# Moving a load of x behind the spectral blocks, reordering copies in the opening chunks, shortening a taps operation and repeating products

## The chip, the cores and the metric

One core of one Trainium2 chip. The metric is the device time of one execution in microseconds: the median of the runs, 957.55 us before the change (three runs, 956.13 to 961.07). Names of engines: PE is TensorE's matmul, PEld its weight load, DVE is VectorE, ACT ScalarE, POOL GpSimd, SP SyncE (which issues the DMAs here).

## The reference

x has the shape (8, 64, 64, 64): batch, channels, two image axes. Two layers follow one another; each adds a convolution of the channel-normalised x and then a small mixture of experts.

```python
x = x + _L0_conv_ref(_ln_c(x), L0_conv_kernel_base)      # spectral: fft, 32x32 modes mixed over channels, inverse
t = _to_tokens(x)
t = t + _L0_ffn_ref(_ln_t(t), ...)                       # 8 experts, the best 2 per token, softmax-weighted
x = _from_tokens(t, x)
x = x + _L1_conv_ref(_ln_c(x), L1_conv_kernels)          # depthwise, 29x29 taps
t = _to_tokens(x)
t = t + _L1_ffn_ref(_ln_t(t), ...)
return _from_tokens(t, x)
```

## The kernel before, in words

One program, five instruction streams written out by hand, one for each engine; each runs in its own order and waits on semaphores. x stays in a region X of on-chip memory, 128 partitions by 256 token tiles of 64 channels. A region R3 and a region R1 hold what the stages need in turn.

**Start and spectral stage.** SyncE loads x twice at the start, by rows (for the statistics, into X) and by channels (for TensorE). TensorE transforms along one axis (line 1453) and the other (line 1470), 16 groups. The mixing stage multiplies the modes with 8 steps of 17 spectral matrices each: SyncE loads the raw pieces of a step (two DMAs a step, line 407), steps 0 to 2 when the transform has left the place free (waits at 402 to 405), later ones when an earlier step's low halves are made; ScalarE makes the high halves (line 1172), VectorE the low ones (line 747), TensorE multiplies (line 1492, up to six small matmuls for each matrix). Between the pieces of step 2 and those of step 3, SyncE waits until the last rows are measured and issues x once more, now in the layout by tokens, in four DMAs into X (line 414), since X is free from there on. After step 7 it issues the experts' weights (line 417). Then come transposes (line 1558), the inverse along one axis (line 1570) and along the other (line 1707); VectorE and GpSimd add its results onto X (lines 1069 and 561) and wait for x by tokens before the first one.

**Token stages.** Each layer handles its 256 tiles in 8 chunks of 32, a chunk in 16 pairs of tiles. A pair `p` of chunk `k`: TensorE computes the products of two tiles with seven experts (`expert_pair`, two matmuls of 448 columns for each tile, lines 1605 and 1606) into one of two PSUM areas; VectorE weighs them by the gates (`weigh_pair`, line 904); GpSimd adds the weighed parts of two pairs (lines 571 and 581); TensorE sums these four tiles with the residual (`sum_quad`, lines 1616 to 1625) and ScalarE copies each two such sums back to X (`copy_sum`, line 1291). Products of pair p+2 wait until pair p is weighed.

Beside the pairs of a chunk the next chunks are prepared, eight tiles (a quarter of a chunk) at a time: VectorE measures (`stats_part`, line 660); ScalarE normalises into one PSUM bank, in two halves of four tiles (`normalise`, line 1249), and takes the high half (line 1261); VectorE makes the low half (`low_parts`, line 844), and only then may ScalarE normalise the next quarter; TensorE turns the eight tiles (`turn_tokens`, line 1583); ScalarE copies the turned tokens out of PSUM (`copy_parts`, lines 1278 and 1279), and only then may TensorE turn the next quarter; TensorE computes the router's logits (`route`, lines 1593 and 1594); VectorE makes the gates in 15 steps (`gate_part`, lines 862 to 892). At which pair each of these happens stands in tables. For the opening chunk (chunk 0) of each layer they are

```python
START_NORMS = {1: (1, 2), 3: (1, 3), 5: (2, 0), 8: (2, 1), 12: (2, 2)}
START_LOWS = {1: (1, 1), 3: (1, 2), 5: (1, 3), 7: (2, 0), 10: (2, 1), 14: (2, 2)}
START_TURNS = {0: (1, 0), 3: (1, 1), 5: (1, 2), 7: (1, 3), 9: (2, 0), 13: (2, 1)}
FIRST_ROUTE = (2, 5, 7, 9)
```

where (1, 2) is quarter 2 of chunk 1. ScalarE's order within a pair is set by `start_chunk` (line 1318), TensorE's by the one at line 1647. Before chunk 0 of each layer its own gates are made (VectorE's 15 steps in a row), while TensorE has done the products of pair 0 and, after the turn of quarter (1, 0), those of pair 1.

At pair 13 of layer 0's opening chunk VectorE also makes the low half of the convolution's taps (`taps_low`, line 946, its instruction at line 950), from `taps_f32` and the copy that ScalarE made (line 1316). SyncE then writes the taps to DRAM in 128 shifted copies, paced by the pairs weighed (line 426). Each half holds 2412 columns in rows of 38; the 29x29 taps lie in one region of it, and all the rest is zero.

**Convolution** (455 to 685 us): a loop over channels, TensorE at line 1692. Layer 1's token stage follows, and the results are stored.

Of the kernel before, what the change touches and what calls it, by code (L numbers as in the profile page):

```python
# [15 lines left out]
B, C, H, W = 8, 64, 64, 64  # L16
# [6 lines left out]
NT = HB * WB * B  # L23
BO, BP, B2 = 2, 2, 2
BH, BQ = 2, 4
KS = 29
NE = 8
KRING = 3
PITCH = 38
# [4 lines left out]
CENTRE = 31 * PITCH + 23  # L34
TAP_SCALE = 256.0
# [32 lines left out]
def metaformer(nc, x_chan, x_rows, x_tok, spec_pairs, spec_last, dft, dft16, inv_h, inv_c, ident, ident16,  # L68
               experts0, experts1, rank, taps, out):
    ctx = ExitStack()  # L70
    with ctx:
# [3 lines left out]
        def sem(name):  # L75
            return ctx.enter_context(nc.semaphore(name))
# [6 lines left out]
        X = sb("X", NT * C)  # L83
# [63 lines left out]
        taps_f32 = R1[:, 5120:5120 + TAPS]  # L147
        taps_16 = R1[:, 7680:7680 + TAPS // 2].bitcast(F16)
# [20 lines left out]
        x_in = sem("x_in")  # L169
        piece_measured = sem("piece_measured")  # L170
# [98 lines left out]
        START_NORMS = {1: (1, 2), 3: (1, 3), 5: (2, 0), 8: (2, 1), 12: (2, 2)}  # L269
# [2 lines left out]
        START_GATES = {9: (0, 1), 10: (2, 3), 11: (4, 5), 12: (6, 7), 13: (8, 9), 14: (10, 11), 15: (12, 13, 14)}  # L272
        START_PARTS = (2, 3, 4, 4, 5, 6, 7, 8)
        START_EXP = 13
        NORM_AHEAD, LOW_AHEAD, TURN_AHEAD = 3, 3, 2
        COPY_AT, SUM_LAG, QUAD_LAG = 1, 2, 3
        GATES_AT = {7: (0, 1), 8: (2, 3), 9: (4, 5), 10: (6, 7), 11: (8, 9), 12: (10, 11), 13: (12, 13, 14)}
# [12 lines left out]
        UNITS = ((0, 0, 32), (0, 32, 64), (1, 0, 32), (1, 32, 64), (2, 0, 64), (3, 0, 64))  # L290
# [69 lines left out]
        def _(sp):  # L360
# [40 lines left out]
            for t in range(NSTEP):  # L401
                if t < 3:
                    sp.wait_ge(c_dft, 20 + 2 * t)
                else:
                    sp.wait_ge(k_low, 2 * (t - 2))
                for r in BLOCKS:
                    sp.dma_start(k_raw[t % 3][r], spec_pairs[:, PER_STEP * t:PER_STEP * t + PER_STEP, :]
                                 ).then_inc(k_in[t % 3], 16)
                if t == 2:

                    sp.wait_ge(piece_measured, len(UNITS))
                    for i in range(4):
                        n = NT * C // 4
                        sp.dma_start(X[:, i * n:(i + 1) * n], x_tok[:, i * n:(i + 1) * n]).then_inc(x_in, 16)

            wait_c_dft_low(sp, 32)
            sp.dma_start(raws_at[0], experts0).then_inc(raw_in, 16)

            sp.wait_ge(inv2, 32)
            for r in BLOCKS:  # L420
# [236 lines left out]
        def _(dve):  # L657
# [288 lines left out]
            def taps_low():  # L946

                dve.wait_ge(taps_step, 1)
                r = BLOCKS[1]
                dve.scalar_tensor_tensor(out=taps_16[r], in0=taps_f32[r], scalar=TAP_SCALE, in1=taps_16[r],  # L950
                                         op0=ALU.mult, op1=ALU.subtract).then_inc(taps_step, 1)

            def plane_stats(lo, hi):
# [167 lines left out]
        def _(act):  # L1121
# [117 lines left out]
            def normalise(layer, k, q, j, tiles=range(8)):  # L1239

                n = layer * NCHUNK + k
                if 0 in tiles:
                    if j == 0:
                        act.wait_ge(tok_step, (n + 1) * TOK_STEPS)
                    if layer or j or k:
                        act.wait_ge(tok_low, n * 4 + j)
                for t in tiles:
                    at = 8 * j + t
                    last = act.activation(xn_psum[:, t * C:(t + 1) * C], X[:, bass.ds(k * CT * C + at * C, C)],  # L1249
                                          ACT.Identity, bias=small[2 * q][:, at:at + 1],  # L1250
                                          scale=small[2 * q + 1][:, at:at + 1])
                if 7 not in tiles:
                    return
                last.then_inc(tok_normed, 1)
                if layer or k:
                    act.wait_ge(across, n * 4 + j - 3)
                act.wait_ge(tok_normed, n * 4 + j + 1 - 4 * layer)
                take_high(j, xn_psum)
# [11 lines left out]
            def copy_parts(layer, k, q, j):  # L1270

                n = (layer * NCHUNK + k) * 4 + j
                act.wait_ge(across, n + 1)
                if layer or not isinstance(k, int) or k >= 2:
                    act.wait_ge(summed, (layer * NCHUNK + k - 2) * NOCT + j + 1)
                src = bank[4 + j % 2] if layer and k == 0 else bank[4]
                at = slice(8 * j * P, 8 * (j + 1) * P)
                act.copy(u[q][:, at].bitcast(F32), src)
                act.copy(vh[q][0:64, at].bitcast(F32), src[0:64]).then_inc(parts_copied, 1)
# [38 lines left out]
            def start_chunk(layer):  # L1318
                for p in range(NPAIR):
                    if p % 4 == COPY_AT and p >= 4 * SUM_LAG:  # L1320
                        copy_sum(layer, 0, p // 4 - SUM_LAG)
                    if p in START_NORMS:
                        k, j = START_NORMS[p]
                        normalise(layer, k, k % 2, j, range(0, 4))
                    if p - 1 in START_NORMS:
                        k, j = START_NORMS[p - 1]
                        normalise(layer, k, k % 2, j, range(4, 8))
                    if p in START_TURNS:
                        k, j = START_TURNS[p]
                        copy_parts(layer, k, k % 2, j)  # L1330
                    if p == 2:
                        root_seed(layer, 2, 0)
                    if not layer and p == 10:
                        taps_high()
                    if p == START_EXP:
                        exp_second(layer, 1)
                    if p == ROOT_AT:
                        root_seed(layer, 3, 1)
# [43 lines left out]
            for g in range(32):  # L1382
                if g in POOLED:
                    n = POOLED.index(g)
# [60 lines left out]
        def _(pe):  # L1445
# [149 lines left out]
                if j == 3:  # L1595
                    mm.then_inc(logits_ready, 1)

            def expert_pair(layer, k, q, p):
                n = (layer * NCHUNK + k) * NPAIR + p
                if not (isinstance(k, int) and k == 0 and layer == 0 and p < 2):  # L1600
                    pe.wait_ge(y_used, n - 1)
                for i in range(2):
                    t = 2 * p + i
                    dst = pair[p % 2][:, i * EC:i * EC + EW]
                    pe.matmul(dst, u[q][:, t * P:(t + 1) * P], wa[:, 0:EW], start=True, stop=False)  # L1605
                    mm = pe.matmul(dst, vh[q][:, t * P:(t + 1) * P], wb[:, 0:EW], start=False, stop=True)  # L1606
                mm.then_inc(y_ready, 1)
# [39 lines left out]
            def start_chunk(layer):  # L1647
                for p in range(NPAIR):
                    if p % 2 == 0 and p >= 2 * QUAD_LAG:
                        sum_quad(layer, 0, 0, p // 2 - QUAD_LAG)  # L1650
                    expert_pair(layer, 0, 0, p)
                    if p in START_TURNS:
                        k, j = START_TURNS[p]
                        turn_tokens(layer, k, k % 2, j)
                    if p in FIRST_ROUTE:
                        route(layer, 1, 1, FIRST_ROUTE.index(p))
# [135 lines left out]
```

## Time and profile before

| what | us |
|---|---|
| median of three runs | 957.55 |
| profiled execution, its own time | 955.84 |
| its span (first to last instruction) | 954.1 |
| TensorE busy (matmuls) | 850.6, 89% |
| VectorE busy | 774.4, 81% |
| GpSimd busy | 567.5, 59% |
| ScalarE busy | 506.9, 53% |
| granted TensorE clock, mean | 0.936 |

All views come from the one profiled execution; times in them count from the span's start. "Granted clock" 1.00 is 2.4 GHz, 0.50 is 1.2 GHz. In a timeline a row is the start, the length, the engine, the line, the operation, what it writes and reads, the shapes and the count of merged instructions; in brackets how long the engine was idle before and what ended that. "Issue" stands for time in which an engine waited for nothing that the profile shows. A busy share is an average over stages with different limits, so the stages that the change touches are read one by one.

### The profile page before, as it was taken

How to read it: one execution, taken by the hardware profiler on the slowest of the kernel's cores; microseconds unless marked ns; L12 is line 12 of the kernel's file. 1: busy time of each engine (PE TensorE's matmuls, PEld its weight loads, DVE VectorE, ACT ScalarE, POOL GpSimd, SP SyncE). 2: the span in 40 equal slices, each digit the busy share in tenths (PEclk: the TensorE clock that was granted, in tenths of full speed). 3: DMA queues.
4: the chain of work that ended last, by engine and by line, in shares of the span. 5: the costliest groups of instructions: out<-in, count | busy, mean ns of one | idle time of the engine just before them, and what ended most of it. 6: DMA issues, size and time to landing. Idle time of an engine off the chain costs nothing.

```text
span 954.1 us, 24392 instructions
## 1 busy us (share of the span) xinstructions
PE 850.6 (89%) x9482; PEld 699.1 (73%) x9482; DVE 774.4 (81%) x1421; ACT 506.9 (53%) x1051; POOL 567.5 (59%) x504
## 2 busy tenths in 40 slices
PE   6997888677999998996899999999658999999998
PEld 6996877645676666654899999999635666667665
DVE  5768698888999989999787677774787999998884
ACT  2467485786667766211444444444168676676511
POOL 3780203157798887796654334330216888889888
PEclk9997577988999999999899999999959999999999
DMA  9997100103777776683787877888000010101101
GB/s 377 355 294 258 50 1 2 40 15 153 281 311 300 301 300 274 280 323 122 265 282 253 286 264 259 274 275 264 13 1 13 33 46 24 45 24 45 46 40 49
DMA packets 48291, 163.09 MB, mean 171 GB/s; under 512 B 9424, under 2 KB 9936, under 8 KB 46032
## 3 DMA queue, kind: packets, MB, share of 16 engines
q1 hardware_dynamic: 48208, 161.96, 46.7%
q8 instruction: 55, 0.90, 0.4%
q14 instruction: 28, 0.23, 0.1%
HBM read 93.46 MB, written 68.49 MB: 170 GB/s over the span
## 4 chain that ended last, share of the span: by engine, by line
PE 50%; DVE 31%; POOL 6%; issue 5%; DMA 3%; ACT 3%; SPq 1%; POOLq 0%; DVEq 0%; ACTq 0%
PE pair L1692 23%; DVE R L904 11%; PE pair L1619 5%; PE pair L1605 5%; PE pair L1606 4%; DMA X<-x_rows 3%; PE pair L1616 3%; DVE R L844 3%; PE pair L1492 3%; POOL R L571 3%; DVE R L660 2%; PE pair L1583 2%; DVE R L833 2%; DVE work L660 2%; ACT pair L1249 1%
## 5 line engine op out<-in xcount | busy, mean ns | idle before, releaser
L904 DVE TENSOR_TENSOR R<-pair,R 128x896 f32<-128x896 f32 x256 | 275.1, 1082 | 41.8 <-PE pair L1606 40.6
L571 POOL TENSOR_TENSOR R<-R 128x768 f32<-128x768 f32 x128 | 231.9, 1812 | 85.8 <-DVE R L904 76.7
L1692 PE MATMUL pair<-R 128*128 (+4 forms) x2880 | 226.8, 242 | 9.8 <-DVE R L982 9.2
L1692 PEld LDWEIGHTS pair<-R 128*128 128x128 f16 x2880 | 223.9, 98 | 12.9 <-issue 10.5
L1249 ACT ACTIVATE pair<-X,work 128x64 f32<-128x64 f32 x480 | 166.7, 394 | 97.1 <-DVE R L844 94.6
L1605 PE MATMUL pair<-work,R 128*128 128x448 f16 x512 | 185.0, 361 | 22.4 <-DVE R L904 20.9
L1606 PE MATMUL pair<-work,R 128*128 128x448 f16 x512 | 184.4, 360 | 0.0
L581 POOL TENSOR_TENSOR R<-R 128x512 f32<-128x512 f32 x128 | 164.9, 1288 | 10.0
L997 DVE COPY R<-R 128x1152 f32<-128x1152 f32 x64 | 93.1, 1455 | 64.9 <-PE pair L1692 64.3
L1367 ACT COPY R<-R 128x1152 f32<-128x1152 f32 x64 | 81.9, 1282 | 117.4 <-PE pair L1692 117.4
L1619 PE MATMUL pair<-R,ident_sb 128*128 128x256 f32 x496 | 128.4, 381 | 0.0
L623 POOL TENSOR_TENSOR R<-X,work 128x1024 f32<-128x1024 f32 x15 | 43.9, 2929 | 103.5 <-DVE R L988 90.4
L1605 PEld LDWEIGHTS pair<-work,R 128*128 128x128 f16 x512 | 50.7, 99 | 73.7 <-DVE R L904 42.3
L1619 PEld LDWEIGHTS pair<-R,ident_sb 128*128 128x128 f32 x496 | 95.0, 191 | 13.1
L660 DVE BATCH_NORM_STATS2 work<-X 128x6 f32<-128x128 f32 x384 | 84.9, 282 | 14.4 <-DMA X<-x_rows 14.4
L1616 PE MATMUL pair<-X,inv_h_sb 128*128 128x256 f32 x248 | 79.7, 403 | 0.0
L1291 ACT ACTIVATE X<-pair 128x512 f32<-128x512 f32 x62 | 36.0, 580 | 73.8 <-PE pair L1625 73.8
L1606 PEld LDWEIGHTS pair<-work,R 128*128 128x128 f16 x512 | 50.9, 99 | 30.7 <-issue 2.0
L1583 PE MATMUL pair<-ident_sb,R 128*128 128x128 f16 x512 | 42.9, 232 | 33.9 <-DVE R L844 27.1
L1583 PEld LDWEIGHTS pair<-ident_sb,R 128*128 128x128 f16 x512 | 36.1, 104 | 48.2 <-DVE R L844 30.4
L1453 PE MATMUL pair<-dft_sb,R 128*128 128x68 f32 x256 | 56.1, 422 | 9.1 <-DMA R<-x_chan 9.1
L1453 PEld LDWEIGHTS pair<-dft_sb,R 128*128 128x128 f32 x256 | 55.2, 333 | 9.3 <-issue 8.9
(137 smaller groups left out, 1292.7 us busy)
## 6 DMA issues: line engine op xcount, KB each, us to landing
taps_halves<-R SPq DMA_DIRECT2D x128, 458.5 KB, 3.3
R<-taps_halves SPq DMA_DIRECT2D x64, 917.0 KB, 4.8
X<-x_tok SPq DMA_DIRECT2D x4, 2048.0 KB, 17.8
out<-X SPq DMA_DIRECT2D x15, 512.0 KB, 2.6
R<-spec_pairs SPq DMA_DIRECT2D x16, 272.0 KB, 5.4
X<-x_rows SPq DMA_DIRECT2D x4, 1024.0 KB, 10.6
R<-x_chan SPq DMA_DIRECT2D x4, 1024.0 KB, 13.7
X<-x_rows SPq DMA_DIRECT2D x2, 2048.0 KB, 27.3
```

What stands on the lines that cost most here:

```text
L571: pool.tensor_tensor(pr[:, :, 192:384], pr[:, :, 0:192], pr[:, :, 192:384], ALU.add).then_inc(half_ready, 1)
L581: pool.tensor_tensor(w, pr[:, :, 192:320], pr[:, :, 320:448], ALU.add).then_inc(quarter_ready, 1)
L660: return dve.bn_stats(out_.rearrange("p t k -> p (t k)"), rows.rearrange("p t c -> p c t"))
L904: dve.tensor_tensor(pr.rearrange("p t (e c) -> p t e c", c=C), pair[p % 2][:, :].rearrange("p (t e c) -> p t e c", t=2, c=C)[:, :, 0:NE - ...
L1249: last = act.activation(xn_psum[:, t * C:(t + 1) * C], X[:, bass.ds(k * CT * C + at * C, C)], ACT.Identity, bias=small[2 * q][:, at:at + 1 ...
L1453: mm = pe.matmul(c_dft_bank(n)[:, j * 68:(j + 1) * 68], xb[:, (4 * n + j) * P:(4 * n + j + 1) * P], dft_sb[:, :], start=True, stop=True)
L1583: mm = pe.transpose(out_[:, t * P:(t + 1) * P], parts[j][:, t * P:(t + 1) * P], ident16_sb[:, :])
L1605: pe.matmul(dst, u[q][:, t * P:(t + 1) * P], wa[:, 0:EW], start=True, stop=False)
L1606: mm = pe.matmul(dst, vh[q][:, t * P:(t + 1) * P], wb[:, 0:EW], start=False, stop=True)
L1616: pe.matmul(bank[7][:, 256 * half:256 * (half + 1)], ident_scaled, X[:, bass.ds((k * NQUAD + g) * 256, 256)], start=True, stop=False)
L1619: pe.matmul(bank[7][:, 256 * half:256 * (half + 1)], ident_sb[:, :], w[:, :, j, :], start=False, stop=False)
L1692: mm = pe.matmul(acc[:, y0:y1, x0:x1, :], blocks[i % 2][:, ks, 2 - y, 1 - x, :], src[:, y0 + y:y1 + y, x0 + x:x1 + x, :], start=(ks == 0 a ...
```

## The change

Four edits. SyncE issues the four DMAs of x by tokens after all spectral pieces and the experts' weights, no longer between steps 2 and 3. In the opening chunks ScalarE does the second half of a normalisation and the copy of turned tokens before the first half of the next normalisation, no longer after it. `taps_low` covers the 29x29 region alone (64 partitions by 29 rows of 29, rows 38 apart). TensorE writes the same products of pair 0 five times over, and those of pairs 11, 13 and 15 twice, in the opening chunk of both layers; the results are the same and the last writing signals.

```diff
+        TIMES = {0: 5, 11: 2, 13: 2, 15: 2}
...
-                if t == 2:
-
-                    sp.wait_ge(piece_measured, len(UNITS))
-                    for i in range(4):
-                        n = NT * C // 4
-                        sp.dma_start(X[:, i * n:(i + 1) * n], x_tok[:, i * n:(i + 1) * n]).then_inc(x_in, 16)
 
             wait_c_dft_low(sp, 32)
             sp.dma_start(raws_at[0], experts0).then_inc(raw_in, 16)
+            sp.wait_ge(piece_measured, len(UNITS))
+            for i in range(4):
+                n = NT * C // 4
+                sp.dma_start(X[:, i * n:(i + 1) * n], x_tok[:, i * n:(i + 1) * n]).then_inc(x_in, 16)
...
                 r = BLOCKS[1]
-                dve.scalar_tensor_tensor(out=taps_16[r], in0=taps_f32[r], scalar=TAP_SCALE, in1=taps_16[r],
+                first = CENTRE - KS // 2 * (PITCH + 1)
+                f32, f16_ = (m[r, first:first + KS * PITCH].rearrange("p (x y) -> p x y", y=PITCH)[:, :, 0:KS]
+                             for m in (taps_f32, taps_16))
+                dve.scalar_tensor_tensor(out=f16_, in0=f32, scalar=TAP_SCALE, in1=f16_,
                                          op0=ALU.mult, op1=ALU.subtract).then_inc(taps_step, 1)
...
-                    if p in START_NORMS:
-                        k, j = START_NORMS[p]
-                        normalise(layer, k, k % 2, j, range(0, 4))
                     if p - 1 in START_NORMS:
                         k, j = START_NORMS[p - 1]
                         normalise(layer, k, k % 2, j, range(4, 8))
                     if p in START_TURNS:
                         k, j = START_TURNS[p]
                         copy_parts(layer, k, k % 2, j)
+                    if p in START_NORMS:
+                        k, j = START_NORMS[p]
+                        normalise(layer, k, k % 2, j, range(0, 4))
...
-            def expert_pair(layer, k, q, p):
+            def expert_pair(layer, k, q, p, times=1):
...
-                for i in range(2):
+                for i in [*range(2)] * times:
...
-                    expert_pair(layer, 0, 0, p)
+                    expert_pair(layer, 0, 0, p, TIMES.get(p, 1))
```

## Rows read from the trace of the kernel before

**Rows 1.** The page, chain of waits that ended last, shares by engine.

```profile
PE 50%; DVE 31%; POOL 6%; issue 5%; DMA 3%; ACT 3%; SPq 1%; POOLq 0%; DVEq 0%; ACTq 0%
```

**Rows 2.** TensorE in the mixing stage: timeline; then waits of 84 to 102 us (us, times, longest).

```profile
82.50 3.88 PE L1492 MATMUL pair<-R 128*128 128x16 f16 x143 [1.50 <-DVE R L729]
89.23 3.56 PE L1492 MATMUL pair<-R 128*128 128x16 f16 x128 [2.85 <-issue]
...
101.25 13.49 PE L1492 MATMUL pair<-R 128*128 128x16 f16 x487 [0.70 <-issue]
...
PE pair L1492 <- issue: 4.2, 4, 2.8
```

**Rows 3.** DMA queues in 62 to 80 us: packets, MB, share of 16 engines.

```profile
q8 instruction: 1, 0.02, 0.4%
```

**Rows 4.** The loads of x by tokens, by source line; the experts' load, SyncE's timeline.

```profile
L414 SPq DMA_DIRECT2D X<-x_tok x4: 432/436/584, 56.4 to 58.0; - x4
...
DMA to landing us min/median/max: 11.1/17.8/26.8
...
96.02 0.52 SPq L417 DMA_DIRECT2D R<-experts  x1
```

**Rows 5.** TensorE's timeline, the turn at pair 5 of each opening chunk.

```profile
204.28 0.61 PE L1583 MATMUL pair<-ident_sb,R 128*128 128x128 f16 x8 [2.35 <-ACT R L1279]
...
721.09 0.61 PE L1583 MATMUL pair<-ident_sb,R 128*128 128x128 f16 x8 [3.36 <-ACT R L1279]
```

**Rows 6.** VectorE's waits, 203.5 to 217 and 717 to 735 us (total, times, longest); timeline.

```profile
DVE R L844 <- ACT R L1261: 2.4, 2, 1.3
DVE R L904 <- PE pair L1606: 1.6, 3, 0.7
...
DVE R L904 <- PE pair L1606: 3.3, 3, 2.1
...
722.95 0.69 DVE L844 TENSOR_TENSOR R<-pair,R 128x512 f16<-128x512 f32 x1 [1.27 <-ACT R L1261]
```

**Rows 7.** Busy time by stretch: PE, PEld, DVE, ACT, POOL, granted clock, DMA share, GB/s.

```profile
190.00:200.20 10.20, 6.70 (x44) 3.68 (x45) 9.28 (x18) 7.42 (x21) 3.01 (x2) 0.50 0.23 49
...
231.00:237.80 6.80, 4.66 (x48) 3.53 (x49) 5.29 (x12) 3.95 (x10) 4.62 (x4) 0.50 0.99 385
...
688.40:715.60 27.20, 14.37 (x145) 9.19 (x146) 24.11 (x64) 16.68 (x43) 5.34 (x14) 0.50 0.00 1
```

**Rows 8.** First products of both layers: TensorE's timeline; chain of waits (start, us).

```profile
192.37 1.03 PE L1583 MATMUL pair<-ident_sb,R 128*128 128x128 f16 x8 [4.14 <-DVE R L844]
...
707.61 1.04 PE L1583 MATMUL pair<-ident_sb,R 128*128 128x128 f16 x8 [3.50 <-DVE R L844]
...
212.09 0.19 PE pair L1605
...
710.12 0.93 DVE R L904
```

**Rows 9.** VectorE's timeline, first addition onto x by tokens.

```profile
151.68 0.69 DVE L1069 TENSOR_TENSOR X<-X,pair 128x512 f32<-128x512 f32 x1 [1.63 <-PE pair L1707]
```

**Rows 10.** VectorE's timeline, chunk 1 of each layer: weighing of pairs 0 and 2.

```profile
233.03 1.09 DVE L904 TENSOR_TENSOR R<-pair,R 128x896 f32<-128x896 f32 x1
...
239.61 1.09 DVE L904 TENSOR_TENSOR R<-pair,R 128x896 f32<-128x896 f32 x1 [2.47 <-PE pair L1606]
...
746.55 1.09 DVE L904 TENSOR_TENSOR R<-pair,R 128x896 f32<-128x896 f32 x1
...
751.23 1.09 DVE L904 TENSOR_TENSOR R<-pair,R 128x896 f32<-128x896 f32 x1 [1.34 <-PE pair L1606]
```

**Rows 11.** Timelines of VectorE and GpSimd at the low half of the taps.

```profile
224.75 3.59 DVE L950 SCALAR_TENSOR_TENSOR R<-R 64x2412 f16<-64x2412 f32 x1
...
224.00 1.81 POOL L571 TENSOR_TENSOR R<-R 128x768 f32<-128x768 f32 x1 [0.41 <-DVE R L904]
225.89 3.57 POOL L581 TENSOR_TENSOR R<-R 128x512 f32<-128x512 f32 x1
```

## The prediction

> **What bounds the kernel now.** I read the chain of waits first. It has no single owner: TensorE holds half of it, VectorE a third, and 5% is "issue", time in which an engine stood for no reason that the profile names [rows 1]. So I went to the three places that the diff touches, each by its own timeline.
>
> The first is the stage that mixes the spectral blocks (line 1492, 82.5 to 114.7 us). TensorE runs it without competition, but it stands four times, each time for "issue": 4.2 us in all, of which 2.85 are the first, at 86.38, and 0.70 the last; the two between share some 0.6 [rows 2]. From the end of one stand to the next there are 128 matmuls, with their weight loads 256 instructions, and the queue named "instruction" moves packets of 0.02 MB [rows 3]. I read the stands as a block of instructions that comes late. The 2.85 fell while x by tokens (four transfers, issued at 56.4 to 58.0, the last landing 26.8 us after its issue, so near 84.8) and the spectral pieces held up behind it were still in flight; the small ones fell beside spectral pieces alone [rows 2, 4].
>
> The second is the opening chunk of each layer (from 187 and 702 us). There ScalarE normalises four columns, copies the turned tokens, and normalises four more; TensorE waits 2.35 us (layer 0) and 3.36 us (layer 1) for the copy at line 1279 before the turn at pair 5 [rows 5]. VectorE, which paces the chunk, then waits for TensorE's products, three times in each layer: 1.6 us in all in layer 0, 3.3 in layer 1, besides twice for ScalarE's normalised columns, 2.4 in layer 0 and about as much in layer 1 [rows 6].
>
> The third is the granted clock. It is 0.5 (1.2 GHz) in 190 to 200 us, 231 to 237.8 and 688.4 to 715.6 [rows 7]. Before the first fall TensorE had run out of work after pair 0 and stood 4.14 us in all [rows 8].
>
> **The change, part by part.**
>
> *x by tokens behind the blocks.* SyncE's queue now issues the five pairs of pieces of steps 3 to 7 and the experts first, then x. The experts went out at 96.02 [rows 4]; the pieces come a little sooner, so x starts near 95.5 and lands 20 to 28 us later (8 MB; its last transfer took 26.8 with other pieces in between). The first reader needs it at 151.68 [rows 9]: some 28 us of cover, cost nothing; without that cover VectorE's additions would be late one for one. The wait on the measured rows, moved along, is over long before, and behind x on the queue stand only the taps, which wait for the end of the inverse stage.
> What it gives: the 2.85. What it costs: x now flies while TensorE mixes and asks for a block every 3.56 us. With the stall gone, requests fall near 97.8, 101.4, 105.0 and 108.5; the last would show only near the stage's end, so I count three and a half. No row shows a block fetched by a fast-running TensorE beside x alone. The ends: 0 (x's big transfers leave gaps), or 2.85 each, as beside x's tail. I take 0.70, the nearest row: the worst under well-filled queues without the jam of x and the pieces held up behind it. Stands after: 0.6 + 3.5 × 0.70 = 3.05 against 4.2, **a gain of 1.1**; the ends are a gain of 3.6 (0.6 left) and a loss of 7.8 (0.6 + 4 × 2.85 = 12.0).
> On this the Trainium skill has a rule, in "Runtime: NRT & Kernel Launch", section Instruction fetch mechanics: instructions come in blocks of 256, the next while the present one runs, and crossing a block costs little because it is mostly hidden. The spacing in this trace agrees with the 256; the 2.85 speaks against "hidden". By that rule of the Trainium skill the stage would not change at all, and the sum below would have 1.1 less of gain.
>
> *Products of pair 0 five times.* 16 more products; one takes 0.19 us of the chain at 2.4 GHz [rows 8], so 3.0 us in layer 0, in the 4.14 us in which TensorE waits for the turn: nothing on the path. In layer 1, at 1.2 GHz and so at twice that for one, 16 × 0.375 = 6.0 us, from 704.1 (707.61 less the 3.50 of waiting) to 710.1; the turn could go at 707.61, and VectorE, held by the gates, weighs pair 0 from 710.12 [rows 8]. If the clock rises during these 20 dense products, they end near 708 and cost nothing, as I take it; if not, pair 1 comes some 0.6 us late. The faster clock that follows gives little: VectorE waits for ScalarE and its own statistics there, at most 0.2.
>
> *Copies ahead of the first four columns* (pairs 3 and 5 only; at the other pairs the two do not meet). The work of ScalarE stays the same and so do the ends of its normalisations, but TensorE gets the copy some 1.4 us sooner, so turn, route, sum and the products of pairs 6, 8 and 10 move up. In layer 0 the three waits for TensorE, 1.6, go, and 0.4 of the second wait for ScalarE, since that copy no longer stands behind a normalisation that waits for VectorE: **2.0**. In layer 1 3.3 go; next late is ScalarE with the columns of chunk 2, which VectorE would meet 0.9 too early: 2.4. Ends: nothing in either layer, or all of the waits for TensorE and half of those for ScalarE, 2.8 and 4.5.
>
> *Pairs 11, 13 and 15 twice.* 4 × 0.19 = 0.76 us each. TensorE has slack there, since VectorE's gates come later than its products, but in layer 1 pair 14 comes behind two repeats and would be about 0.35 late once VectorE is 2.4 sooner. So **2.05** are left of layer 1.
>
> *Taps from their region.* 64 × 841 elements in place of 64 × 2412. The instruction took 3.59 us from 224.75, but GpSimd's addition at line 571, begun at 224.00, lasted 1.81, to 225.81, and its next one took 3.57, to 229.46, just past VectorE's end at 228.34 [rows 11]: the two engines took turns. So 1.06 was waiting and 2.53 work; 841 / 2412 of that is 0.88. GpSimd is at the same point of its own work in the new order, so I keep the 1.06: **a gain of 1.65**, up to 2.7 if the wait goes too, and 1.0 if the 29 short rows cost twice as much per element.
>
> *The clock at 231.* VectorE finishes the gates sooner, and TensorE has repeats at pairs 13 and 15: the stands that came before the fall grow shorter. I take it that the clock stays at 2.4 GHz. From the weighing of the next chunk's pair 0 to that of pair 2 it takes 239.61 − 233.03 = 6.58 us in layer 0 and, at full clock, 751.23 − 746.55 = 4.68 in layer 1 [rows 10]: **a gain of 1.9**, or nothing.
>
> *Sum.* 1.1 + 2.0 + 2.05 + 1.65 + 1.9 = 8.7. The chunks after the opening ones and the convolution start from these points and keep their lengths, so nothing takes it back. The profiled execution took 955.84 (span 954.1): 947.1. It lies 1.7 below the median of the runs, 957.55, which is what is compared: **948.8 us**.
>
> **Rivals.**
> *x stands in front of TensorE's instructions.* If a fetch has to wait for all that is queued on the engines, the one asked near 97.8 comes with x, at 116 to 122, and TensorE stands 15 to 20 us. The rest gives 7.6 and the old stands 3.6: from 11.2 us of standing the change loses; at 17.5 it ends 6.3 slower, at 963.9. For it: the 2.85 ended only as the held-up pieces landed. Against: a fetch came in at its time while x alone filled the queues from 62 to 80 (one packet on the instruction queue there [rows 3]) and TensorE ran on. Chance 0.05.
> *Every block as late as the worst*: a loss of 7.8 against 7.6 of gains, 957.8, no change. Chance 0.10.
> *The copies give nothing*, because ScalarE's normalisations, whose ends stay, set VectorE's pace: 4.05 less, 952.8. For it: the first wait for ScalarE in each layer stays as it is [rows 6]. Against: the waits behind them name TensorE. Chance 0.13.
> *The stand was no fetch* and the mixing keeps its length: 949.9. The equal spacing is against it. By the Trainium skill's rule on fetches, above, this is what should come. Chance 0.12.
>
> **How the numbers follow.** The forecast has 0.60. Its own ends (mixing 3.6, taps 2.7, or no gain from the clock and one copy) give 945 to 953. A difference of 0.5%, 4.8 us, is about what a measurement tells from none: below 952.8 is faster, above 962.3 slower. Faster: nearly all of the forecast, the fourth rival, half of the third: 0.76. Slower: the first, 0.05. The rest, 0.19, is the same. For 8 in 10 I take 944.5 to 956.5, which leaves out the first rival and the second.
>
> **What would show it.** Right: no long issue stand near 86, several under 1 us between 97 and 112, line 1492 ending a little before 114; x landing before 125; no wait of TensorE for line 1279 above 1 us; line 950's successor under 2.2 us; clock 1.0 from 226 on, and the two chunks' first weighings to third ones equally long. Wrong: a stand of TensorE of several us after 97, a wait for x at line 1069, or VectorE's waits for line 1606 replaced by as long ones for line 1261.

## The result, and the profile after

The changed kernel takes 960.4 us (median of 12 runs, 957.56 to 961.93); the kernel before, on the same chips, 957.33 (12 runs). The ratio is 1.0027 with a 95% interval of 1.0016 to 1.0038: slower by 0.3%, which is within the 0.5% that the prediction counted as no change, where it forecast 948.8 and a gain. The profiled execution took 960.74 (span 958.8), 4.7 us of span more than before.

The chain of waits has the same owners as before [rows 1], with a little more "issue":

```profile
PE 51%; DVE 29%; POOL 6%; issue 6%; ACT 4%; DMA 3%; SPq 1%; POOLq 0%; DVEq 0%; ACTq 0%
```

TensorE's timeline in the mixing stage (line 1494 after), then the stage's row in the list of waits (us in total, times, longest); they answer to [rows 2]:

```profile
82.94 3.82 PE L1494 MATMUL pair<-R 128*128 128x16 f16 x143 [2.26 <-DVE R L728]
87.51 3.57 PE L1494 MATMUL pair<-R 128*128 128x16 f16 x128 [0.74 <-issue]
91.25 3.56 PE L1494 MATMUL pair<-R 128*128 128x16 f16 x128 [0.17 <-issue]
96.07 3.58 PE L1494 MATMUL pair<-R 128*128 128x16 f16 x128 [1.26 <-issue]
103.37 3.79 PE L1494 MATMUL pair<-R 128*128 128x16 f16 x128 [3.72 <-issue]
109.84 3.79 PE L1494 MATMUL pair<-R 64*64 64x16 f16 x128 [2.69 <-issue]
116.05 3.58 PE L1494 MATMUL pair<-R 128*128 128x16 f16 x128 [2.41 <-issue]
121.16 2.91 PE L1494 MATMUL pair<-R 128*128 128x16 f16 x103 [1.52 <-issue]
...
PE pair L1494 <- issue: 12.5, 7, 3.7
```

The 2.85 of before is gone, as foreseen, but now every block of 128 matmuls is late, and the four that fall beside x stand 3.72, 2.69, 2.41 and 1.52 us. The stands grew from 4.2 us to 12.5. The granted clock is not behind it: it is 0.51 in 83.5 to 114 us before and 0.53 after.

What flies beside them: SyncE's timeline, and the landings of x by tokens (line 416), answering to [rows 4].

```profile
94.89 0.52 SPq L412 DMA_DIRECT2D R<-experts  x1
95.45 2.26 SPq L416 DMA_DIRECT2D X<-x_tok  x4
...
DMA to landing us min/median/max: 10.5/17.1/23.3
```

The DMA view by queue (packets, MB, share of 16 engines), for 96.1 to 100.8, 100.8 to 101.5 and 97.5 to 118 us:

```profile
q1 hardware_dynamic: 270, 1.70, 98.0%
...
q1 hardware_dynamic: 16, 0.26, 87.5%
q8 instruction: 1, 0.02, 9.7%
...
q1 hardware_dynamic: 674, 8.58, 100.0%
q8 instruction: 3, 0.05, 1.0%
```

These rows show the mechanism; the starts of the single packets are read from the same trace. TensorE enters a new block at 96.07. No packet of the instruction queue begins until 100.8; the next one begins at 100.87, and the stand ends 2.50 later, at 103.37. The three after it begin at 107.46, 113.60 and 118.70, and their stands end 2.38, 2.45 and 2.46 later. So beside x a block is ready about 2.45 us after its packet begins, and since a block runs 3.56, the packet must begin within about 1.1 of TensorE's entry into the block before it, or TensorE stands. Beside x it begins 4.8, 4.1, 3.8 and 2.65 after that entry: 4.8 + 2.5 − 3.58 is the 3.72 of the first stand.

From the mixing to the end, as the difference to the same point of before (the end of TensorE's mixing, or the start of a weighing at line 903, line 904 before):

| point | after minus before, us |
|---|---|
| mixing ends | +9.33 |
| inverse stages, first weighing of layer 0 | +8.79 |
| pair 8 of layer 0 | +7.18 |
| pairs 10 to 13 of layer 0 | +7.64 |
| pair 14 of layer 0 (behind the taps) | +6.00 |
| chunk 1 of layer 0, pair 2 | +5.38 |
| first weighing of layer 1 | +5.84 |
| pair 6 of layer 1 | +4.12 |
| pair 14 of layer 1 | +4.69 |
| end of the span | +4.72 |

One stage loses 9.33; all the rest together gains 4.6.

The taps (line 952), VectorE's timeline and the weighing behind it, answering to [rows 11]:

```profile
232.39 1.95 DVE L952 SCALAR_TENSOR_TENSOR R<-R 64x841 f16<-64x841 f32 x1
234.38 1.09 DVE L903 TENSOR_TENSOR R<-pair,R 128x896 f32<-128x896 f32 x1
```

In layer 0's opening chunk, waits of 212.3 to 225 us, answering to [rows 6], and TensorE's and VectorE's timelines at pair 10:

```profile
DVE R L843 <- ACT R L1263: 1.9, 2, 1.1
DVE R L903 <- PE pair L1608: 1.2, 1, 1.2
...
PE pair L1618 <- ACT X L1293: 0.8, 1, 0.8
...
221.94 0.67 PE L1618 MATMUL pair<-X,inv_h_sb 128*128 128x256 f32 x2 [0.83 <-ACT X L1293]
...
224.50 1.09 DVE L903 TENSOR_TENSOR R<-pair,R 128x896 f32<-128x896 f32 x1 [1.18 <-PE pair L1608]
```

Two of VectorE's three waits for products are gone. The third, at pair 10, has grown, from 0.70 to 1.18. ScalarE makes the copy of sums (line 1293, before: 1291) between the two halves of a normalisation, in both kernels. It comes 7.72 us later than before (at 221.21, where it came at 213.49), while VectorE at pair 8 is only 7.18 later. TensorE now waits 0.83 for it with its next sum, where it did not wait before, and the products stand behind that sum.

In layer 1 the turn at pair 5 still waits 1.87 us for the copy, where it waited 3.36 [rows 5]:

```profile
725.45 0.61 PE L1585 MATMUL pair<-ident_sb,R 128*128 128x128 f16 x8 [1.87 <-ACT R L1281]
```

The windows (busy time of PE, PEld, DVE, ACT, POOL, granted clock, DMA share, GB/s), answering to [rows 7]:

```profile
190.00:199.90 9.90, 8.16 (x134) 6.04 (x131) 8.28 (x21) 6.43 (x18) 0.00 (x0) 1.00 0.43 97
199.90:210.00 10.10, 6.71 (x52) 3.55 (x52) 8.97 (x17) 8.09 (x23) 3.57 (x3) 0.83 0.15 30
...
237.00:239.10 2.10, 0.00 (x0) 0.00 (x0) 2.00 (x5) 2.10 (x7) 1.35 (x2) 1.00 0.99 393
239.10:242.50 3.40, 3.35 (x45) 2.49 (x46) 2.66 (x6) 1.17 (x3) 1.96 (x3) 0.50 1.00 385
...
727.00:731.00 4.00, 4.00 (x20) 2.22 (x20) 2.33 (x5) 3.91 (x11) 3.52 (x4) 0.57 0.00 0
```

Since layer 0's opening chunk comes 8.8 us later now, the stretch that answers to 190 to 200.2 of before is about 199 to 209. The clock is low there too, but later and for a shorter time: 3.4 us, from 205.0 to 208.4, where it was 10.2. The fall at the end of the chunk is shorter as well (3.4 us) but still there. TensorE's timeline shows what comes before it:

```profile
239.15 0.17 PE L1595 MATMUL pair<-work,R 128*128 128x8 f16 x1 [2.69 <-DVE R L891]
```

TensorE stands 2.69 us, until VectorE has made the gates (line 891), and right behind that, from 239.1, the clock is 0.50. In layer 1 it falls once more at 727, as it did before the change at the same place (at 722.5):

```profile
722.50:725.80 3.30, 3.30 (x17) 2.06 (x16) 1.09 (x3) 2.48 (x7) 2.34 (x2) 0.50 0.00 0
```

### The profile page after: what moved, and what is told of

Its sections match the earlier page's. It is cut to its first block, busy times and chain, and to the rows that moved or that the text cites. A ratio compares the mean times of both kernels' runs of the same rounds, so it can differ in the third digit from the quotient of the medians.

```text
span 958.8 us, 24504 instructions
## 1 busy us (share of the span) xinstructions
PE 857.9 (89%) x9538; PEld 702.2 (73%) x9538; DVE 771.4 (80%) x1421; ACT 506.4 (53%) x1051; POOL 566.8 (59%) x504
## 4 chain that ended last, share of the span: by engine, by line
PE 51%; DVE 29%; POOL 6%; issue 6%; ACT 4%; DMA 3%; SPq 1%; POOLq 0%; DVEq 0%; ACTq 0%
PE pair L1694 24%; DVE R L903 11%; PE pair L1621 5%; PE pair L1607 5%; PE pair L1608 4%; DMA X<-x_rows 3%; PE pair L1618 3%; PE pair L1494 3%; POOL R L570 3%; DVE R L843 3%; DVE R L659 2%; PE pair L1585 2%; DVE R L832 2%; DVE work L659 2%; ACT pair L1251 2%
## 5 line engine op out<-in xcount | busy, mean ns | idle before, releaser
L1607 PE MATMUL pair<-work,R 128*128 128x448 f16 x540 | 194.4, 360 | 20.5 <-DVE R L903 18.9
L1608 PE MATMUL pair<-work,R 128*128 128x448 f16 x540 | 193.9, 359 | 0.0
L1607 PEld LDWEIGHTS pair<-work,R 128*128 128x128 f16 x540 | 53.4, 99 | 73.7 <-DVE R L903 39.4
L1608 PEld LDWEIGHTS pair<-work,R 128*128 128x128 f16 x540 | 53.6, 99 | 33.7 <-issue 2.7
```

## The experiments

Theory of the first runs: x in flight delays TensorE's instruction blocks, and that alone makes the change a loss. Its rival: the stands come from what else was changed, or from the pieces and experts that x no longer holds up.

**e1, the move of x alone** (the kernel before, with line 414's block behind the experts):

```diff
-                if t == 2:
-                    sp.wait_ge(piece_measured, len(UNITS))
...
             sp.dma_start(raws_at[0], experts0).then_inc(raw_in, 16)
+            sp.wait_ge(piece_measured, len(UNITS))
+            for i in range(4):
...
```

> The kernel before with the load of x moved behind the spectral pieces and the experts, and nothing else. Theory (x in flight starves TensorE of instructions): the mixing stage shows the same row of stands as the changed kernel, about 12 us in all in place of 4.2, it ends near 123.5 instead of 114.6, and nothing later takes it back: 8 to 9 us slower than before, ratio near 1.009. Rival (the stands come from elsewhere, x moved costs nothing): ratio 1.000, mixing ends near 114.

Measured: 964.46 us against 957.93, ratio 1.0063 (1.0043 to 1.0083), 6 us slower. Waits of the mixing stage and TensorE's timeline beside x:

```profile
PE pair L1490 <- issue: 11.8, 7, 3.2
...
101.41 3.79 PE L1490 MATMUL pair<-R 128*128 128x16 f16 x128 [3.17 <-issue]
107.89 3.80 PE L1490 MATMUL pair<-R 64*64 64x16 f16 x128 [2.69 <-issue]
114.37 3.58 PE L1490 MATMUL pair<-R 128*128 128x16 f16 x128 [2.68 <-issue]
```

The move by itself makes the stands and the whole loss, a little less than the 8 to 9 us expected: the mixing ends 7.65 later and the span 6.85.

**e2, everything but the move of x** (the changed kernel, x issued between steps 2 and 3 as before):

```diff
+                if t == 2:
+                    sp.wait_ge(piece_measured, len(UNITS))
+                    for i in range(4):
...
```

> The changed kernel with the load of x put back between the pieces of steps 2 and 3; the three edits of the opening chunks stay. Theory: the mixing stage is that of before (4.2 us of stands, the first near 2.9), and the opening chunks keep what the trace of the changed kernel shows, 3.4 us in layer 0 and 1.1 in layer 1: about 4.1 us faster than before, ratio near 0.996. Rival (the repeats or copies cost what they give and the trace misleads): ratio 1.000.

Measured: 953.45, ratio 0.9945 (0.992 to 0.9969), 5.3 us faster. Its profiled execution had late blocks of its own (3.31 at the same place as before, then 1.54 and 2.62 beside pieces and experts), which shows that the place of before is not safe either; even so, from the first weighing of layer 0 to the end it gains 3.1 us of span, where the changed kernel gains 4.1.

**e3, x behind the mixing** (the changed kernel; SyncE waits for the last mixed product before it issues x):

```diff
             sp.dma_start(raws_at[0], experts0).then_inc(raw_in, 16)
+            sp.wait_ge(mixed, NMIX)
             sp.wait_ge(piece_measured, len(UNITS))
```

> The changed kernel with one more wait ahead of the load of x: it starts when the last spectral product is written. Theory: in the mixing stage only the stands beside the spectral pieces stay, under 2 us in all, it ends near 112; x flies beside the transposes and the first inverse, where TensorE waits for copies anyway, lands near 133 and is needed near 148; about 6.5 us faster than before, ratio near 0.993. Rival (TensorE is short of instructions there whatever flies): stands of over 8 us in all, ratio near 1.003. Second rival (the cost only moves into the stages behind): mixing ends near 112 but the first inverse ends no earlier than with x in its old place, ratio near 0.996 or above.

Measured: 951.99, ratio 0.9923 (0.9894 to 0.9953), 7.4 us faster than before. TensorE's timeline in the mixing, and the DMA queues of 101.1 to 114 us:

```profile
91.36 3.56 PE L1495 MATMUL pair<-R 128*128 128x16 f16 x128 [1.00 <-issue]
95.91 3.58 PE L1495 MATMUL pair<-R 128*128 128x16 f16 x128 [0.99 <-issue]
101.02 11.06 PE L1495 MATMUL pair<-R 128*128 128x16 f16 x384 [1.53 <-issue]
112.50 2.91 PE L1495 MATMUL pair<-R 128*128 128x16 f16 x103 [0.42 <-issue]
...
q8 instruction: 3, 0.05, 1.6%
```

Once the experts have landed nothing but instructions moves, and 384 matmuls pass without a stand. The stands that are left are 4.4 in all, and all but the last (0.42) fall beside the pieces and the experts; I had expected less than 2, and an end of the mixing near 112 where it came at 115.42. Nothing is paid later for the later load: x is issued at 115.5, the last part lands 21.9 us after its issue, and the transposes, at whose side it flies, end 0.02 sooner than before.

**e4, one part of x in flight at a time** (each of the four loads waits for the landing of the one before):

```diff
             for i in range(4):
                 n = NT * C // 4
+                if i:
+                    sp.wait_ge(x_in, 16 * i)
```

> The changed kernel with each of the four transfers of x issued only when the one before has landed. In the changed kernel the stand shrinks as transfers land: 3.72, 2.69, 2.41, 1.52. Theory (a block waits behind as many packets as transfers are in flight): with one in flight each stand is at most about 1.5, 5 to 6 us in all, the mixing ends near 117 to 118, and the whole is 1 to 2 us faster than before, ratio 0.998 to 0.999. Rival (any flow of x does it): the stands stay at 2.4 to 3.7 and the ratio near 1.003, or a little more as x takes longer.

Measured: 955.94, ratio 0.998 (0.9963 to 0.9997). Waits of the stage, then its timeline:

```profile
PE pair L1496 <- issue: 8.2, 5, 4.0
...
103.06 7.53 PE L1496 MATMUL pair<-R 128*128 128x16 f16 x256 [3.99 <-issue]
112.72 6.38 PE L1496 MATMUL pair<-R 128*128 128x16 f16 x231 [2.13 <-issue]
```

Fewer blocks are late, but those that are late are about as late as with all four in flight. At the first, 3.99, the last pieces and the experts flew as well. At the second, 2.13, a single part of x flew and nothing else: its packet began 3.7 us after TensorE entered the block ahead, as late as the 3.8 and 4.1 of the changed kernel. Between the two parts, with the queues nearly empty, one packet began after 1.1 and its block came without a stand. So the theory is wrong (stands of 1.5 at most, 5 to 6 in all; measured 8.2), and that the ratio came out at its 0.998 is luck.

**e5, x in 16 loads** of a quarter of the width, at the changed kernel's place:

```diff
-            for i in range(4):
-                n = NT * C // 4
+            for i in range(16):
+                n = NT * C // 16
```

(The two waits for x count 16 landings instead of four.)

> The changed kernel with the load of x cut into 16 transfers, each a quarter as wide, issued in a row at the same place. Theory 1 (a late block waits for some packets of x ahead of it): with packets a quarter as long the stands of 2.4 to 3.7 us beside x shrink to under 1.5 each and the mixing ends near 116. Theory 2 (any traffic that fills the queues does it, whatever the packet): the stands stay at 2.4 to 3.7 and the mixing ends near 123.

Measured: 960.66, ratio 1.0026 (1.0012 to 1.0039), the changed kernel's time. Waits of the mixing stage, and the DMA queues of 96.5 to 121 us:

```profile
PE pair L1494 <- issue: 12.4, 7, 2.9
...
q1 hardware_dynamic: 2493, 9.05, 94.5%
q8 instruction: 4, 0.07, 1.1%
```

About the same bytes in 3.7 times as many packets (2493 for 9.05 MB here, 674 for 8.58 MB in 97.5 to 118 us of the changed kernel) leave the same stands, 12.4 us against 12.5. The size of a packet is not what delays an instruction packet.

**e8, x behind the mixing and nothing else** (the kernel before, with the wait of e3):

```diff
-                if t == 2:
-                    sp.wait_ge(piece_measured, len(UNITS))
...
             sp.dma_start(raws_at[0], experts0).then_inc(raw_in, 16)
+            sp.wait_ge(mixed, NMIX)
+            sp.wait_ge(piece_measured, len(UNITS))
+            for i in range(4):
...
```

> The kernel before with the load of x moved behind the mixing stage, and nothing else. Theory: the stands of the mixing stage fall from between 4 and 8 us to between 2 and 4.5 and nothing pays for it later: 1.5 to 4 us faster, ratio 0.996 to 0.9985. Rival (x's traffic costs the stages behind the mixing what the mixing gains): ratio 1.000.

Measured: 956.28, ratio 0.9983 (0.9973 to 0.9993), 1.6 us faster; the stands are 3.8, and the mixing ends 0.19 sooner than in the profiled execution of before. This place is worth 7.7 us against the changed kernel's (0.9983 against e1's 1.0063), but little against that of before. Its profiled execution has 1.1 us more of span than that of before, all of it lost in the opening chunks and just behind, where the clock fell at other times (from 228.6 to 238.9, for example, where before it was low from 231 to 237.8). So behind the mixing two traces can differ by a microsecond or two with the same instructions there.

The next four look at the other parts, with x behind the mixing throughout.

**e6, no products repeated** (e3 with an empty table):

```diff
-        TIMES = {0: 5, 11: 2, 13: 2, 15: 2}
+        TIMES = {}
```

> The kernel of the run with x after the mixing, with every product written once. Theory (the repeats only raise the clock where VectorE does not wait for TensorE): the low clock of 190 to 200 us and of 691 to 718 us comes back, VectorE's points to pair 5 of both layers stay within 0.2, and the whole changes by less than 1.5 us: ratio to before 0.992 to 0.994. Rival (the repeats carry the gain of the opening chunks): 2 us or more are lost, ratio 0.995 or above.

Measured: 952.58, ratio 0.9945 (0.9928 to 0.9963). Beside e3's 0.9923 (0.9894 to 0.9953) no difference shows. At pair 14 of layer 0 the two stand within 0.01 us of one another, and the clock falls behind it in both (0.86 in 226 to 231 us in e3, 0.92 in e6). In the traces the repeats take and give: from the weighing of chunk 1's pair 0 to that of pair 2 it takes 7.37 us in e3 and 5.99 in e6 in layer 0, and 4.69 and 6.03 in layer 1. Over the whole neither a gain nor a cost of the repeats can be told from nothing; the ratio lies between the theory's range and the rival's.

**e7, the new wait removed and the clock held** (e3; the copy of sums at pair 8 instead of 9; repeats also at pairs 4 and 5, and pair 0 of chunk 1 in layer 0 written four times):

```diff
-        TIMES = {0: 5, 11: 2, 13: 2, 15: 2}
+        TIMES = {0: 5, 4: 2, 5: 2, 11: 2, 13: 2, 15: 2}
...
-                    if p % 4 == COPY_AT and p >= 4 * SUM_LAG:
+                    if p in (8, 13):
...
-                    expert_pair(layer, k, q, p)
+                    expert_pair(layer, k, q, p, 4 if layer == 0 and k == 1 and p == 0 else 1)
```

> The kernel with x after the mixing, and in the opening chunks the first copy of a sum goes one pair earlier (ahead of the normalisation it stood behind), pairs 4 and 5 are written twice, and pair 0 of layer 0's second chunk four times. Theory: in layer 0 TensorE no longer waits 0.8 us for line 1293's copy before the sum at pair 10 (0.5 to 1.0 gained), and in both layers the stretches of low clock behind the opening stands go (layer 0 from 230 to 236, 0.6 to 1.5 gained; layer 1 from 711 to 721, 0.3 to 1.0): 1.5 to 3 us below the run with x after the mixing alone, ratio to before 0.989 to 0.991. Rival (those waits are covered by VectorE's own work): ratio 0.992.

Measured: 947.8, ratio 0.9894 (0.9866 to 0.9922). Its windows over the end of layer 0's opening chunk and over layer 1's, then VectorE's waits of 202 to 216 us and its weighing of pair 2 of chunk 1:

```profile
229.60:236.40 6.80, 6.80 (x82) 5.20 (x81) 5.50 (x14) 2.33 (x7) 4.48 (x4) 1.00 1.00 385
700.80:745.00 44.20, 39.18 (x377) 26.22 (x375) 38.91 (x79) 33.40 (x90) 30.48 (x30) 1.00 0.03 13
...
DVE R L844 <- ACT R L1264: 1.9, 2, 1.1
DVE R L904 <- PE pair L1609: 0.2, 1, 0.2
...
233.35 1.09 DVE L904 TENSOR_TENSOR R<-pair,R 128x896 f32<-128x896 f32 x1 [1.29 <-PE pair L1609]
```

The wait for pair 10 is gone, the clock is 1.00 through both stretches, and from the weighing of chunk 1's pair 0 to that of pair 2 it takes 233.35 − 228.78 = 4.57 us where it took 6.58 [rows 10].

**e9, the same kernel again**, since one of e7's four executions took 1403.87 us and the others 947.22 to 948.22:

> The combined version once more: x after the mixing, the sum's copy at pairs 8 and 13, repeats at pairs 0, 4, 5, 11, 13, 15 of the opening chunks and at pair 0 of chunk 1. Its first measurement had a median of 947.8 with one execution far outside. If that one was a disturbance, this gives 947 to 949 in every execution, ratio 0.988 to 0.991; if the version has a second way to run, some executions come out far above 950 again.

Measured: 948.16 (947.68 to 948.9, four executions), ratio 0.99 (0.9883 to 0.9916). The long one did not come back in these four, so nothing speaks for a second way to run; what it was stays open.

**e10, e7 without the repeats in the opening chunks** (an empty table; the four writings in chunk 1 stay):

> The combined version without any repeat in the opening chunks; the four writings of pair 0 of chunk 1 in layer 0 stay. Theory 1 (the repeats of the opening chunks only raise the granted clock, and nothing on the path uses it): layer 0's opening chunk ends within 0.3 us of the combined version's, the clock holds 1.00 from 226 to 236, the total is 947 to 949. Theory 2 (they keep the clock up at the end of the chunk): the clock falls to 0.50 near 228 to 233 and 1.4 to 2 us are lost between the weighings of pairs 0 and 2 of chunk 1, so 949.5 or more.

Measured: 947.78, ratio 0.9891 (0.9874 to 0.9907). Windows of 206 to 226, 226 to 236 and, in layer 1, 700 to 745 us:

```profile
216.00:226.00 10.00, 8.17 (x66) 5.39 (x65) 9.80 (x16) 7.46 (x19) 8.00 (x8) 1.00 0.10 41
226.00:236.00 10.00, 9.58 (x107) 6.57 (x106) 8.53 (x17) 5.45 (x14) 6.94 (x8) 1.00 1.00 386
...
700.00:715.00 15.00, 10.83 (x79) 6.05 (x80) 13.68 (x33) 11.52 (x34) 7.04 (x8) 0.62 0.00 0
...
725.00:745.00 20.00, 17.26 (x157) 11.85 (x156) 16.70 (x31) 12.23 (x33) 16.32 (x16) 0.91 0.07 27
```

Layer 0's opening chunk comes to the same point as e7's (both 3.8 us shorter than before from its first weighing to pair 15), and the clock stays at 1.00 from 226 on: there the four writings in chunk 1 and the earlier sums hold it without the repeats (no run parts these two). In layer 1 the clock is lower without them (0.62, where e7 has 1.00), yet the opening chunk ends as early; 1.5 us are lost once, at chunk 1, where it falls near 740. By the medians the two versions are the same, and both beat the kernel before by 1%.

## Why the prediction was wrong, step by step

**x by tokens behind the blocks: the step that failed.** The prediction read the stands rightly as late blocks, saw that x would now fly beside the requests, at the right time (issued at 95.45, forecast 95.5), and gave both ends of the price. It then took 0.70 for each, "the nearest row", from blocks fetched beside spectral pieces, and "three and a half" of them. Measured were four, of 3.72, 2.69, 2.41 and 1.52, together 10.34 us where 2.45 were counted, and 2.17 from the three blocks before them where 0.6 stood. The mixing lost 9.33 where a gain of 1.1 was forecast: the 8.3 of stands, 0.44 of a later start, and two blocks that ran 3.79 instead of 3.56. The end that the prediction had set aside, 2.85 a block and a loss of 7.8, was nearly right. The row taken was the nearest in engine and line, but not in what mattered. Its block was fetched in a short burst of pieces and experts: the DMA share was 0.00 in 94.9 to 96.0 us, 0.77 in 96.0 to 101.0 and 0.02 after that, while x keeps the queues full without a pause (0.99 in 95.5 to 118.5). It was a low draw besides: the block fetched beside the experts stood 0.70 there, but 1.53 in e3, 1.52 in e8 and 2.62 in e2. The one row from the end of a long full stretch (1.01 in 56.0 to 82.5) was the 2.85, and it should have been the value. The prediction's reading of it needs one correction: by 82.5 the last packet of x had begun, and until 86.4 only the held-up pieces flew (0.74 MB). So what delays a block need not be x itself. The prediction gave this case 0.10.

The Trainium skill, "Runtime: NRT & Kernel Launch", section Instruction fetch mechanics, has the next block fetched while the present one runs, and the crossing "mostly hidden". Its block of 256 instructions agrees here (128 matmuls with their weight loads); the hiding does not, with 12.5 us of stands in one stage. What hid a fetch in these runs is queues that are free: in e3, 384 matmuls passed unhindered once no load was in flight.

**"Some 28 us of cover" for x** was right: its slowest part landed 23.3 us after an issue near 97, the first addition comes at 160, and no wait for x shows. The cost lay not with x's readers but with what shares its way, and the step asked only for the readers.

**The copies in layer 0**, 2.0 forecast, gave 1.15: 1.61 up to pair 8, less 0.46 at pair 10, where the next sum now waits for the copy of sums. The prediction kept ScalarE's work where it was and let TensorE's sum "move up" with the rest; it did not ask what the sum itself waits for, which is ScalarE's copy of the sums before it (line 1291). With that copy one pair sooner (e7) the same step gives 2.11.

**The copies in layer 1**, 2.05 forecast with the cost of pair 14 taken off, gave 1.15: 1.47 up to pair 13, less 0.32 at pair 14 (forecast 0.35). Most of what was missing lies at pair 6: its products stand in the 727 to 731 us in which the clock is 0.57. Before the change the clock fell at the same place (722.5 to 725.8); the prediction's list of falls leaves it out, and counts all 3.3 of the waits as gone, also what that fall costs. In e7, where the clock stays at 1.00, the chunk gains 2.35 at pair 6 against the changed kernel's 1.72 (2.36 in e2 and e10 too, where the clock is up there; 1.64 in e3, where it is not), 2.57 up to pair 13, of which 0.50 at pair 10 by the earlier copy of sums, and loses 0.32 at pair 14.

**The taps**: 1.64 measured, 1.65 forecast. The instruction took 1.95, in all nine runs that have it, where 1.06 + 0.88 = 1.94 was worked out. So the part that stayed is as long as GpSimd's addition still had to run when the instruction began (232.39 to 233.45, 1.06), and the short rows cost nothing extra. (The low end of the range should have been 0.77, 1.65 − 0.88, and not 1.0.)

**The clock at 231**: 1.9 forecast, 0.63 measured. The prediction let the stands before the fall grow shorter. The one of 2.9 us ahead of the products of pair 15 went, but the one that directly precedes the fall is the wait for the gates, behind the repeats of pair 15, which do not reach over it: 2.7 us before, 2.69 after. Even the 0.63 is not firm. In the five kernels with the same edits here the stretch took 5.91 to 6.22 us where the clock was low for 3.4 (the changed kernel, e4, e5), and 7.37 and 7.56, longer than before, where it was low for 6.8 (e3, e2). The price was right: where the clock was held (e7), that stretch gained 2.01.

**Five writings of pair 0** cost nothing, as forecast. They filled most of the stand before the turn (1.11 us left of 4.14), and the clock was low for 3.4 us there and not for 10.2; nothing on the path used it, since with the repeats (e3) VectorE weighs pair 5 at the same distance from the first weighing as without (e6), to within 0.01 us in both layers.

So the terms behind the mixing were right in kind, and all four (the copies in either layer, the taps, the clock) also in size once their conditions were met: e7 is 8.5 us of span below the kernel before, nearly the 8.7 forecast. But e7 needed edits that the change did not have (x behind the mixing, the earlier copy of sums, more repeats), so this bears out the sizes of the terms and not the forecast for the change. Rival by rival: the fetch did not wait for the whole of x (the first late packet began 5.4 us after x's first issue, while the last part of x, issued by 97.7, took up to 23.3); the blocks were as late as the worst, the second rival, whose 957.8 became 960.4: in the traces the mixing lost 9.3 where it counted 7.8, and the other parts gave 4.6 where it counted 7.6; the copies did give something; and the stands were fetches.

What stays open is where an instruction packet waits. It is not behind one large packet (e5), and not behind all that is queued, since three come through while x flies and the fourth at its end. That a fixed number of bytes has to pass first would fit e4 and e5 both; it was not tried.

## What to carry to other kernels

A large load can cost more than its readers' waits: beside a stretch where an engine issues short instructions without pause, it delays the blocks of instructions that this engine fetches, here with stands of 2.6 us for each block on average. Put such a load beside a stage where no engine stands for instructions, if it still lands before its first reader (e3, 7.4 us faster than before, against 2.6 us slower). When a price must be taken from a row, choose the row by the resource that is short, here queues that stay full, and not by the line it stands on; and look for a second such row, since one trace gives one draw (0.70 to 2.62 us for the block beside the experts).

## What the runs showed of the hardware

- In the mixing, with loads of x in flight, a stand for instructions ended 2.3 to 2.5 us after its packet on the instruction queue began (all four of the changed kernel, 2.38 to 2.50), while the packet itself took about 1.1. The rest of the delay is before the packet begins: 2.65 to 4.8 us after TensorE entered the block ahead of it.
- That delay did not depend on packet size (3.6 to 4.1 us in e5), and with one load of 2 MB in flight it was as long as with several (3.7 in e4, against 3.8 and 4.1). With nothing else in flight it was 1.1 (e3, the packet after 101.02).
- A taps instruction of 64x841 took 1.95 us and one of 64x2412 3.59 [rows 11]: less than in proportion. The two give a fixed part of 1.07 us, and in both cases GpSimd's addition, begun 0.75 us earlier, had 1.06 still to run; no run took that addition away.
- The granted clock fell from 1.00 to 0.50 right behind a stretch of 2.69 us in which TensorE did nothing, and with the same edits at that place the low stretch lasted 3.4 us in some kernels and 6.8 in others. In kernels that differ elsewhere it fell at other points of the same stage (727 us in the changed kernel, near 740 in e10, nowhere in layer 1's opening chunk in e7).
